# Score products of a head pair in opposite row halves of the array, interleaved in different banks; repeat copies of splits on GpSimd

## The reference

```python
x = x + 0.5 * ffn(layernorm(x), ...)
x = x + attn(layernorm(x), ...)
x = x + 0.5 * ffn(layernorm(x), ...)

# attn: xn = x * rsqrt(mean(x*x) + 1e-6) * norm_w
q = (xn @ Wq.T + bq).reshape(B, T, H, hd).transpose(0, 2, 1, 3)     # k, v alike; hd = 8
scores = einsum('bhqd,bhkd->bhqk', q, k) / sqrt(hd)
scores = where(causal, -inf, scores)
out = einsum('bhqk,bhkd->bhqd', softmax(scores), v)
return xn + (out merged over heads) @ Wo.T + bo
```

## Time and profile before

| | |
|---|---|
| median of 3 runs | 320.19 us |
| the profiled execution's own time | 319.46 us |
| its span | 317.7 us |
| busy in the span: TensorE, its weight loads | 277.9 us (87%), 226.6 us (71%) |
| VectorE, GpSimd, ScalarE | 214.2 us (67%), 178.9 us (56%), 159.3 us (50%) |
| exponentials L723 | 96 of 599 ns |
| reductions L1038, L1042 | 64 of 682 ns, 32 of 690 ns |
| masks L541 | 62 of 645 ns |

### The profile page before, as it was taken

One profiled execution on the slowest core, in us unless ns is written; L12 is line 12 of the kernel. 1 busy time (PEld: TensorE's weight loads), 2 busy tenths in 40 slices (PEclk: granted clock), 3 DMA queues, 4 the chain that ended last, 5 costly groups with the idle time before them and its releaser, 6 DMA issues.

```text
span 317.7 us, 7990 instructions
## 1 busy us (share of the span) xinstructions
PE 277.9 (87%) x2396; PEld 226.6 (71%) x2396; DVE 214.2 (67%) x691; ACT 159.3 (50%) x389; POOL 178.9 (56%) x319
## 2 busy tenths in 40 slices
PE   7563999999997876999999999999967699999980
PEld 7563999999996463556666666665646598999970
DVE  3877038887707839997676777876796564888870
ACT  2430066666304844485766657777551106666620
POOL 5577824445625201487777777878747830455561
PEclk9655899999997979799999999999995569999995
DMA  6973131221030730663525422210001134122100
GB/s 170 397 313 119 51 96 38 68 68 39 25 105 29 196 118 36 191 187 100 162 72 151 135 82 71 68 54 5 4 11 43 51 108 99 43 75 66 32 19 0
DMA packets 34387, 29.37 MB, mean 92 GB/s; under 512 B 4108, under 2 KB 28817, under 8 KB 34352
## 3 DMA queue, kind: packets, MB, share of 16 engines
q1 hardware_dynamic: 29696, 23.52, 24.4%
q0 software_dynamic: 2496, 4.27, 4.2%
q10 hardware_dynamic: 2160, 1.14, 1.3%
HBM read 17.08 MB, written 12.55 MB: 93 GB/s over the span
## 4 chain that ended last, share of the span: by engine, by line
PE 57%; POOL 12%; DVE 10%; issue 8%; DMA 5%; ACT 4%; POOLq 1%; SPq 0%; ACTq 0%; DVEq 0%
PE bank L1279 12%; PE bank L1290 11%; PE bank L1207 5%; PE bank L1436 3%; PE bank L1408 3%; PE bank L1384 3%; POOL disp_d L462 3%; POOL pT L541 2%; PE bank L1346 2%; PE bank L1381 2%; POOL row L454 2%; PE bank L1414 2%; PE bank L1389 2%; PE bank L1393 2%; PE bank L1271 2%
## 5 line engine op out<-in xcount | busy, mean ns | idle before, releaser
L723 ACT ACTIVATE pT<-bank 128x512 f32<-128x512 f32 x96 | 56.4, 599 | 34.2 <-PE bank L1414 23.9
L1207 PE MATMUL bank<-zero 128*128 128x128 f32 x298 | 45.4, 325 | 8.5 <-DVE rowi L916 4.6
L1207 PEld LDWEIGHTS bank<-zero 128*128 128x128 f32 x298 | 43.9, 238 | 9.0 <-DVE rowi L916 4.7
L1279 PE MATMUL bank<-xsT,ew 128*128 128x128 f32 x368 | 48.8, 276 | 0.2 <-ACT xsT L621 0.2
L1290 PE MATMUL bank<-experts,hT 128*128 x368 | 49.0, 276 | 0.0
L1038 DVE TENSOR_REDUCE mh<-bank 128x2 f32<-128x512 f32 x64 | 42.1, 682 | 9.2 <-PE bank L1384 8.9
L1279 PEld LDWEIGHTS bank<-xsT,ew 128*128 128x128 f32 x368 | 44.7, 192 | 0.7 <-ACT xsT L621 0.5
L1290 PEld LDWEIGHTS bank<-experts,hT 128*128 128x128 f32 x368 | 44.8, 192 | 0.5 <-issue 0.3
L541 POOL TENSOR_SCALAR_AFFINE_SELECT pT<-pT 128x512 f32<-128x512 f32 x62 | 39.9, 645 | 9.1 <-ACT pT L723 8.9
L627 ACT ACTIVATE hT<-bank,ew 128x128 f32<-128x128 f32 x92 | 28.8, 364 | 28.9 <-PE bank L1279 28.9
L923 DVE TENSOR_SCALAR hT<-bank,ew 128x128 f32<-128x128 f32 x92 | 28.0, 346 | 20.7 <-PE bank L1279 19.3
(11 more groups left out here) (133 smaller groups left out, 479.9 us busy)
## 6 DMA issues: line engine op xcount, KB each, us to landing
sp_d<-spl SPq DMA_DIRECT2D x32, 192.0 KB, 2.5
experts<-in_experts SPq DMA_DIRECT2D x8, 578.0 KB, 8.9
qz<-sp_d SPq DMA_DIRECT2D x32, 96.0 KB
ks<-sp_d SPq DMA_DIRECT2D x32, 96.0 KB
xs_sb<-disp_d SPq DMA_DIRECT2D x46, 66.0 KB, 1.9
row<-in_x SPq DMA_DIRECT2D x4, 256.0 KB, 5.6
row<-x_d SPq DMA_DIRECT2D x4, 256.0 KB, 4.3
disp_d<-pad ACTq DMA_DIRECT2D x12, 66.0 KB, 1.9
```

Source lines behind the costliest of these rows:

```text
L723: act.activation(pT[:, u, :], bank[2 + u % 2][:, :], ACT.Exp, scale=SCALE).then_inc(a_e, 1)
L1207: pe.matmul(bank[b][:, 0:P], zero[:, :], zero[:, :], start=True, stop=True)
L1279: mm = pe.matmul(bank[2 + 2 * (k % 2) + c // 2][:, (c % 2) * P:(c % 2 + 1) * P], ew[:, k % WRING, c * P:(c + 1) * P], xsT[:, k % 2, :], st ...
```

## The change

The two heads of a pair now lie in rows 0 to 50 and 64 to 114 of `qz` and `ks`, each with its own three maximum rows; no zeros are needed. A unit holds one head of each of two or four pairs: units 0, 1, 4 and 5 are early ones, 2 and 3 late ones. In a step the key-side products of b (head u%2) and the query-side products of b+1 (the other head) are issued in turn, in different row halves and banks, behind the mask of the query side and behind the waits of both. `pv(.., 0)` moves from after unit 4 to after unit 5 and waits for three masks; the masks are those of units (0, 1), 2, 3 and (4, 5). `max_rows` issues two DMAs. The repeat copies move from ScalarE to GpSimd, as 32-bit words, and two fills of `qz` go. The diff, cut to its core:

```diff
-SROWS = 2 * JROWS
-MROW = SROWS
-KROWS = MROW + 3
+KROWS = JROWS + 3
+JBASE = P // 2
-        qz = [sb(f"qz{i}", [P, 2, 2, 4, T], BF16) for i in range(2)]
+        qz = [sb(f"qz{i}", [P, 2, 4, T], BF16) for i in range(2)]
+        def unit(u):
+            late = u in (2, 3)
+            return late, 0 if late else 2 * (u // 4), 4 if late else 2
@@ SP: split_stores waits q_cp >= 2q+2; stack_load rows JBASE * j
             def max_rows(b, k, half):
                 sp.wait_ge(a_mtc, 2 * b + half + 1)
-                sp.dma_start(qz[k][MROW:MROW + 3, half, :, :, :].rearrange("s j i n -> s (j i n)"), mT[:, half, :]
-                             ).then_inc(a_m[half], 16)
+                for j in range(2):
+                    sp.dma_start(qz[k][JBASE * j + JROWS:JBASE * j + KROWS, half, :, :].rearrange("s i n -> s (i n)"),
+                                 mT[12 * j:12 * j + 12, half, :]).then_inc(a_m[half], 16)
@@ GpSimd
-                pool.memset(qz[k][:, :, :, :, :].rearrange("p h j i n -> p (h j i n)").bitcast(F32), 0.0
-                            ).then_inc(static_s, 1)
+            def quad_repeat(q, t):
+                w = width(q)
+                pool.wait_ge((q_s2, q_s1)[t], q + 1)
+                pool.tensor_copy(spl[:, q % SPL, 2, t, 0:w].bitcast(I32), spl[:, q % SPL, 1 - t, t, 0:w].bitcast(I32)
+                                 ).then_inc(q_cp, 1)
+            for q in range(4):
                 ln_scale(1, q)
+            quad_repeat(0, 1)
+            quad_repeat(0, 0)
+            quad_repeat(1, 1)
+            quad_repeat(1, 0)
+            ln_scale(1, 4)
+            quad_repeat(2, 1)
+            quad_repeat(2, 0)
-                pool.wait_ge(a_e, 12 * b + 6 * half + 3 * pp + 2 + late)
+                pool.wait_ge(a_e, 12 * b + 6 * half + (2, 3, 4, 6)[n])
             max_split(0, 0)
+            quad_repeat(3, 1)
+            quad_repeat(3, 0)
+            quad_repeat(4, 1)
             for half in range(2):
+                if half == 1:
+                    quad_repeat(4, 0)
                 step(0, half)
@@ ScalarE: quad_repeat(0) to (4) removed
-                need(act, a_pv, 2 * (2 * b + half - 1) + 1 + u // 3
+                need(act, a_pv, 2 * (2 * b + half - 1) + (1 if u < 2 else 2)
@@ VectorE: max_unit takes one head of 2 or 4 pairs; last_mask by the new units
@@ TensorE
+            def scores_q_mask(b, bh, k, half, u):
+                if u == 0:
+                    pe.wait_ge(a_stk[k][half], 64 * (bh + 1))
+                need(pe, a_mx, 12 * b + 6 * half + u - 1)
+                _, _, heads = unit(u)
+                pe.matmul(bank[u % 2][:, :].rearrange("p (h n) -> p h n", h=heads)[:, :, 512 // heads - P:], ident_b,
+                          maskS.unsqueeze(1).broadcast_to((P, heads, P)), start=True, stop=False, **MM_BANK)
+            def scores_q_part(k, half, u, m):
+                late, p0, heads = unit(u)
+                n = 512 // heads
+                q_, k_ = head(k, half, p0 + m, 1 - u % 2, JROWS)
+                return pe.matmul(bank[u % 2][:, m * n:(m + 1) * n], q_[:, 0:P] if late else q_[:, P:T], k_[:, 0:n],
+                                 start=False, stop=True, **MM_BANK)
+            def scores_k_waits(b, half, u):
+                if u == 0:
+                    pe.wait_ge(a_m[half], 32 * (b + 1))
+                need(pe, a_e, 12 * b + 6 * half + u - 1)
+            def scores_k_part(k, half, u, m):
+                late, p0, heads = unit(u)
+                n = 512 // heads
+                q_, k_ = head(k, half, p0 + m, u % 2, KROWS)
+                return pe.matmul(bank[2 + u % 2][:, m * n:(m + 1) * n], k_[:, P:T] if late else k_[:, 0:P],
+                                 q_[:, T - n:T], start=True, stop=True, **MM_BANK)
+            def scores(b, bh, k, half, u, more):
+                scores_k_waits(b, half, u)
+                if more:
+                    scores_q_mask(b + 1, bh, 1 - k, half, u)
+                for m in range(unit(u)[2]):
+                    mk = scores_k_part(k, half, u, m)
+                    if more:
+                        mq = scores_q_part(1 - k, half, u, m)
+                mk.then_inc(a_st, 1)
+                if more:
+                    mq.then_inc(a_s, 1)
             def pv(b, k, half, pp):
-                pe.wait_ge(a_pm, 8 * b + 4 * half + 2 * pp + 2)
+                pe.wait_ge(a_pm, 8 * b + 4 * half + pp + 3)
             def step(b, bh, k, half, more, first=False):
                 for u in range(6):
-                    scores_k(b, k, half, u)
-                    if more:
-                        scores_q(b + 1, bh, 1 - k, half, u)
+                    scores(b, bh, k, half, u, more)
@@
-                    if u == 4:
+                    if u == 5:
                         pv(b, k, half, 0)
```

More of the change, by code:

```diff
@@ L392, in stack_load @@
                 for j in range(2):
-                    rows_j = slice(JROWS * j, JROWS * (j + 1))
-                    for t, buf in ((0, qz[k][rows_j, half, j, :, :]),
+                    rows_j = slice(JBASE * j, JBASE * j + JROWS)
+                    for t, buf in ((0, qz[k][rows_j, half, :, :]),
                                    (1, ks[k][rows_j, 4 * half:4 * half + 4, :])):
@@ L505, in residual @@
                 i1.then_inc(q_res, 1)
-            for q in range(NU):
-                ln_scale(1, q)
+            def quad_repeat(q, t):
[4 more added lines that the diff above has]
+            for q in range(4):
+                ln_scale(1, q)
+            quad_repeat(0, 1)
[5 more added lines that the diff above has]
+            quad_repeat(2, 0)
             pool.wait_ge(ln_xn[1], NU)
@@ L549, in step @@
                 for n in range(4 if more or half == 0 else 2):
-                    mask(b, half, n // 2, n % 2)
+                    mask(b, half, n)
                     if isinstance(b, int) and b >= 6:
@@ L711, in _ @@
             quad_split2(2)
-            quad_repeat(2)
             quad_copy(4)
@@ L728, in max_copy @@
                 act.wait_ge(a_mt, 2 * b + half + 1)
-                need(act, a_m[half], 16 * b)
+                need(act, a_m[half], 32 * b)
                 act.copy(mT[:, half, :], bank[6][0:24, 0:P].bitcast(BF16)).then_inc(a_mtc, 1)
@@ L1369, in _, with head @@
             maskS = cb[:, C_MS:C_MS + P]
-            def scores_q(b, bh, k, half, u):
-                pp, w = divmod(u, 3)
+            def head(k, half, p_, j, top):
+                return (qz[k][JBASE * j:JBASE * j + top, half, p_, :],
+                        ks[k][JBASE * j:JBASE * j + top, 4 * half + p_, :])
+            def scores_q_mask(b, bh, k, half, u):
                 if u == 0:
@@ L1396, in scores_q @@
-                mm.then_inc(a_s, 1)
-            def scores_k(b, k, half, u):
-                pp, w = divmod(u, 3)
-                if u == 0:
-                    pe.wait_ge(a_m[half], 16 * (b + 1))
-                need(pe, a_e, 12 * b + 6 * half + u - 1)
-                o = bank[2 + u % 2]
-                if w < 2:
-                    pair = 4 * half + 2 * pp + w
-                    ov = o[:, :].rearrange("p (j n) -> p j n", j=2)
-                    mm = pe.matmul(ov, ks[k][0:KROWS, pair, 0:P], qz[k][0:KROWS, half, :, pair - 4 * half, :],
-                                   start=True, stop=True, **MM_BANK)
-                else:
-                    ov = o[:, :].rearrange("p (i j n) -> p i j n", i=2, j=2)
-                    for i in range(2):
-                        pair = 4 * half + 2 * pp + i
-                        mm = pe.matmul(ov[:, i, :, :], ks[k][0:KROWS, pair, P:T],
-                                       qz[k][0:KROWS, half, :, pair - 4 * half, P:T],
-                                       start=True, stop=True, **MM_BANK)
-                mm.then_inc(a_st, 1)
+                _, _, heads = unit(u)
@@ new lines, in scores_q @@
+            def scores_q(b, bh, k, half, u):
+                scores_q_mask(b, bh, k, half, u)
+                for m in range(unit(u)[2]):
+                    mm = scores_q_part(k, half, u, m)
+                mm.then_inc(a_s, 1)
+            def scores(b, bh, k, half, u, more):
+                scores_k_waits(b, half, u)
+                if more:
+                    scores_q_mask(b + 1, bh, 1 - k, half, u)
+                for m in range(unit(u)[2]):
+                    mk = scores_k_part(k, half, u, m)
[4 more added lines that the diff above has]
+                    mq.then_inc(a_s, 1)
```

92 lines of the change are left out of this document (28 added, 64 removed).

## The result

The changed kernel takes **336.69 us** (median of four runs, 335.73 to 339.08) against 320.01 for the kernel before. The medians' quotient is 1.052; the ratio estimated over the runs is 1.054, with a 95% interval of 1.050 to 1.059. It is slower, by 16.7 us where 3.1 were forecast, and far outside the range. Its profiled execution spans 334.6 us, 16.9 more than the one before (317.7).

A forecast was written before the change was run, and what follows sets the result against it. TensorE was taken as the bound, busy 13.25 of 13.33 us a sequence. Terms 2.8 + 1.0 + 0.3 - 1.0 = +3.1 us took the profiled 319.46 to 322.6, forecast as a 323.3 us median; range 316.2 to 328.5.

The forecast's parts named there:

- A unit: TensorE's scores: pairs overlap, but two shape changes of 0.11 us give the doubling back; 0.55 us early, 0.66 late.
- doubt about the weight loads: Slower rival: row halves share the load path, so late units grow by 0.22 us; +4.7 us, 328 us, chance 0.12.
- The loop: Sequences 1 to 4: waits around the moved pv(0) make each sequence 14.05 us against 13.33; +2.8 us.
- T: Time mark in each half: start of VectorE's reduction of unit 2, put at 2.64 us after the half's start.
- landing of the second DMA of the maximum rows: On SP, two DMAs instead of one, landing at T+4.7 at worst: 0, up to 0.3 us per half.
- the moved pv(0): After unit 5 it no longer covers ScalarE's work for the output's turn and projection, and needs three masks.
- The first twelve query-side units: Units without a partner: two shape changes each, mostly hidden by VectorE's reductions; +0.3 us, from 0 to 2.6.
- Sequence 0: First sequence, without turn or projection: 0, between a gain of 0.33 us per half and a loss like the loop's.
- the gain of 0.33 per half: Three units of six, where pv or the maximum's transposes follow, save one 0.11 us shape change each.
- Sequences 5 and 6: After the loop, no turn instruction before a mask, so TensorE's way bounds: +0.5 us each, +1.0 together.
- Sequence 7 to the experts: Last sequence, without query side: 0, between a gain of 0.33 us per half and a loss like the loop's.
- The repeat copies: Front: fewer ScalarE copies bring copy and idle work earlier; -1.0 us, from 0 (late stacks) to -2.4 (full clock kept).

The follow-up runs named there:

- e1: Changed kernel with each unit's query-side product from the same head and row half as its key-side product: 368.7 and 372.3 us.
- e13: Changed kernel with each mask product split into two 64-row products in the row half of its unit's query side: 328.0 us, ratio 1.027.
- e4: Kernel before with only pv(0) moved from after unit 4 to after unit 5, still behind two masks: 326.4 us, ratio 1.023.
- e3: Changed kernel with pv(0) put back after unit 4 and residual pieces behind the third mask: 357 to 361 us.
- e5: Changed kernel with GpSimd's first and third residual pieces behind the third mask instead of the second: 333.7 us, ratio 1.042.
- e6: Changed kernel with the first turn and the projection issued after unit 5 instead of unit 4: 335.8 and 337.3 us.
- e7: Changed kernel with the edits of e5 and e6 together: 334.2 us, ratio 1.048.
- e9: e7 with the maximum's transposes after unit 1 and, from sequence 1 on, split stores behind stack loads: 337.0 us, ratio 1.054.
- e11: Changed kernel with the residual pieces of sequences 5, 6 and 7 shrunk to 2x4 elements of a row: 332.1 us, ratio 1.040.
- e14: e13 with e7's two order edits: 329.1 us, ratio 1.031.
- e15: e14 with the maximum's transposes one unit earlier and split stores behind stack loads: 333.9 and 338.0 us.
- e12: Changed kernel with e8's products on zeros and each mask product of sequence 0 issued twice: 336.0 us, ratio 1.054.
- b2: Kernel before with only the ten repeat copies moved from ScalarE to GpSimd: 319.3 us, ratio 0.996.
- e8: Changed kernel with 16 products on zeros in TensorE's pauses in the twelve query-only units before sequence 0: 335.8 us, ratio 1.046.

## Why the prediction was wrong, step by step

**A unit: right.** Pairs run side by side, each change of shape takes 0.1 us, and a unit 0.54 us where 0.55 was said (e1, e13). For the overlap the forecast set the Trainium skill, "TensorEngine Tiling (Array Packing)", Theoretical Speedup, against the drains. The trace agrees with its factor of up to two for the products: 0.11 us for a pair instead of 0.22. It also agrees with what the same page says under Key Properties, that a change of mode drains the engine; the price, 0.1 us a change, which here equals the gain, is the trace's. The forecast's doubt about the weight loads was answered too: late pairs start every 0.056 us with two loads each, so the loads are not what limits here. The Trainium skill's "TensorE: Matmul & The Clock Gate", LDWEIGHTS, gives columns / 1.2 ns, from which the estimate was 107 ns for each load; no such price shows in that pace.

**The loop: right mechanism, too small.** It is +4.5 us for +2.8. From a half's start to T 2.65 us was measured (198.31 to 200.96) and 2.64 said, and the second halves took 7.0 for 7.06. The first halves failed: from T to T they took 7.2, 7.3, 7.2 and 7.5 us for 6.99, 1.1 us in all. In each of the four, 0.12 of that is pv(0), released late; in the last, the landing of the second DMA of the maximum rows adds some 0.4, where the forecast had "0, up to 0.3 per half". The forecast had no lost clock in the loop either: it is at half until 149.6, and from its first exponential to T sequence 1 needs 2.5 us where sequence 2 needs 1.9. The cost belongs to the moved pv(0) in any layout (e4), which the forecast put down as such but never priced alone.

**The first twelve query-side units: failed.** +0.3 was taken from a range of 0 to 2.6, on the argument that VectorE's reductions hide the changes; +2.8 came. From the first mask to the first exponential it takes 14.8 us in the changed kernel and in six variants that leave these units as they are (e3, e5, e6, e7, e9, e11); it takes 12.9 to 13.4 in those whose units have no changes of shape (e13, e14, e15), though their clock falls in the midst of them as well. So 1.4 to 1.9 of the 2.8 are the changes of shape, which the reductions did not hide. What the rest is stays open.

**Sequence 0: failed.** "0", between the gain of 0.33 per half and a loss like the loop's, met +4.3: 1.4 in the first half and 2.8 in the second. The first goes with the clock, lost with TensorE busy (e12 keeps it and the first half takes 7.2 us for 8.9). In the second TensorE waits 1.29 us for GpSimd's third mask, and e4, with two masks to wait for, is 0.8 over the kernel before. The forecast read the full clock of the earlier trace rows as given, and asked of the clock only what the shorter idle work would do to it.

**Sequences 5 and 6: failed.** +1.0 met +2.7. The move alone makes +1.4 (e4), and e11 takes 1.0 of the rest back by shortening GpSimd's pieces. The forecast took TensorE's way as the bound since the `turn` instructions are gone there, and did not add up GpSimd's queue, where scales stand beside masks and residual pieces.

**Sequence 7 to the experts: failed.** 0 met +3.3, of which 3.1 lie in the first half of the sequence. 2.0 of these are the fall of the clock at 241.7, a term that the forecast did not have. The move costs nothing there (e4), and the remaining 1.0 of the half is in each of the eight variants with the clock full over it. Why the clock falls at that place in some variants and later in others is open.

**The repeat copies: the number right, by luck at the front.** b2 gave the 1 us that was said, with 0.4 to 2.2 as its interval. But the first mask's -0.8 came of the two things that the forecast had set at the ends of its range. The clock was kept, so that the idle work took 2.5 us instead of 4.0, and the stack landed late, so that this won nothing more. The path named, copy and idle work, no longer releases the first mask.

Why e7, e12 and e14 lost at the ends what they won in the loop or in sequence 0 is not settled: a fall of the clock that the changed kernel had not, or had at another place, is in each of these traces, and so are GpSimd's and VectorE's waits in sequence 7, and no run here parts the two.

## What to carry to other kernels

Half-height products side by side paid here only where whole runs of them stayed in one shape: a full-height mask in each unit cost as much as the pairs saved, and moving the mask into the same shape gave back 2.6 of the 4.5 us that the loop had lost. When a group of products is moved, price the move alone, in the kernel before: what it had been covering (here ScalarE's copies) cost by itself as much as the whole change did in the loop. Cost the sequences before and after a loop by their own queues, and ask of the clock wherever TensorE's work changes. Before an experiment's gain is put down to its edit, look in which stretch it lies and whether the clock fell at the same place: 3 of e11's 4 us did not survive that.

## What the runs showed of the hardware

TensorE was granted 1.2 GHz while it was busy all the time: 23.50 of 23.50 us in e1, with half-height products one after the other, and 8.82 of 8.90 us in the changed kernel, where the kernel before, with full-height products, lost the clock there for 3.4 us only. Twelve full-height products of 0.11 to 0.22 us more, with 16 on zeros ahead, held it over all of sequence 0 (e12); the 16 alone did not (e8). The same instructions of sequence 7 took 8.42 us at full clock and 10.45 where the clock fell 5.8 us in. Mask and key-side products of different row halves and different banks started in the same hundredth of a microsecond and took 0.28 us each, as a mask does alone (e13). Ten float32 products on zeros (20 instructions) took 4.02 us with the clock at half for most of it and 2.50 at full clock.
